# A step's transposes in two halves, with half of the products behind each, and the products half a step later

## Chip, cores, metric

One core of a Trainium2 chip. The metric is device time in microseconds; the kernel before takes 1659.14 us (median of three runs, 1657.83 to 1659.40).

## What is computed

A decoder block of a perceiver: `x` is 8 batches x 64 rows x 2048, the context 8 x 1601 x 2048. All in float32.

```python
x = x + xattn(layernorm(x), ctx)        # a = q @ ctx.T; softmax(a) @ ctx
x = x + attn(layernorm(x), w_q, w_k, w_v, w_o)   # causal, 32 heads, 8 kv heads
x = x + ffn(layernorm(x), A_w, B_w, Wq_w, keys)  # 64 gated experts of rank 8
```

The change lies in the first line. Keys and values of this cross attention are both the context itself: for the scores it is needed transposed, for the products (softmax times context) as it lies in memory.

## The kernel before

**Tiling.** A batch is two stages: `x = 0` with 833 keys (six tiles of 128 and an odd one of 65) and `x = 1` with 768 (six tiles). A stage is four steps (`PER`), one for each 512 columns of the model dimension; a step is four chunks (`CHUNKS`) of 128 columns. There are 64 steps (`STEPS`) that transpose and score, and a few behind them. Below, steps of a batch are numbered 0 to 7.

**What TensorE (PE) does in a step**, in the order in which it is written in `cross_tensor` (line 610 on):
- four chunks of transposes (`transpose_chunk`, L623), six or seven tiles each, into one of two PSUM places (`u % UNITS`). ACT copies columns 0 to 511 to `xa_ct` (L442), DVE the others (L577). A chunk waits until the copies of the chunk two before it are through (`first_copied`, `second_copied`). Some steps transpose more in the same places: step 5 the exponentials of the stage just scored (`xa_expo`, L638, and `xa_odd_e`, L641) and step 1 likewise, step 7 the next batch's queries (`xa_xq`, L635), which wait for `q_ready`;
- the products (`product`, L690) that `product_steps` puts in this step;
- the scores (`scores`, L664, L668), which wait for the copies of this step's chunks.

A product of the order ("use") is one key tile for each of two halves of the keys, which go to the two halves of the array's columns. Stage 0 has 14 uses, stage 1 has 12, in four groups (512 columns each) that accumulate in banks 6 and 7. The uses of a stage are spread over four steps that begin one step (`PV_AT`) after its last scores. `GROUP_STEP` is the step of a group's last use, and the work of the other engines is placed by it through `groups_before(t, ago)`.

**The other engines**, each with its own loop over the steps, all in order:
- ACT: four copies of chunks; in step 0 and 4 of a batch the softmax (L424, L427); for each group of this step the copy of the first stage's sum to `xa_acc` (L457) or of the upper half to `xa_low` (L460); in `OUT_NORM_AT` the finished rows are normalized (L466).
- DVE: four copies of chunks (and L579 for exponentials and queries); maxima (L507 to L515); statistics of the previous step's group (`out_row_stats`, L556); in `OUT_LINKS_AT` the chain for the finished rows (L561, L213 to L219, L590); for the next batch's queries statistics in steps 2 to 5 (L480), a chain whose halves stand in steps 5 and 6 (L486, L213 to L219; `CHAIN_AT`), and in step 6 (`NORM_AT`) the four multiplies L490, the last of which sets `q_ready`; last the epilogue of this step's group: `rescale` (L532), `fold` (L538), `finish` (L548). A link waits for the link before it.
- SyncE (SP): for each group of the previous step the reload of its piece of context for the next batch (L363), stores of finished rows, loads of `xq` and `xr`.

```python
            for gh, c in groups_before(t, 1):
                if gh % HALVES == 1 and gh // HALVES != B - 2:
                    out_row_stats(gh // HALVES, c)
            if t in OUT_LINKS_AT:
                some(out_links(), 11)
```

The decoder behind it (attention and experts, some 1,050 us) starts with transposes of the finished rows (L1677) and isn't touched.

Of the kernel before, what the change touches and what calls it, by code (L numbers as in the profile page):

```python
# [37 lines left out]
SIDES, JOINT = 2, 3  # L38
# [3 lines left out]
STAGES = HALVES * B  # L42
CHUNKS, UNITS = 4, 2
PER = DC // CHUNKS
STEPS = STAGES * PER
PV_AT = 1
# [34 lines left out]
def product_steps():  # L81

    at, step_of = {}, {}
    for h in range(STAGES):
        n = USES_OF[h % HALVES]
        for i in range(n):
            t = PER * (h + 1) + PV_AT + (i * PER // n if h < STAGES - 1 else i // JOINT)
            at.setdefault(t, []).append((h, i))
            step_of[h, i] = t
    return at, step_of  # L90


USE_AT, USE_STEP = product_steps()
GROUP_STEP = {(h, c): USE_STEP[h, GROUP_END[h % HALVES][c]] for h in range(STAGES) for c in range(NCOL)}
GROUPS_AT = {}
# [30 lines left out]
def chunk_no(t, u):  # L126

    return CHUNKS * min(t, STEPS) + u


def chunks_at(t):

    return range(CHUNKS if t < STEPS else JOINT if t == E_LAST else 0)


def copies_until(what, h, j):

    return next(chunk_no(t, u) for (t, u), v in SIDE.items() if (what, h, j) in v) + 1
# [83 lines left out]
def cross_attention(nc, stack, x_rows, ctx, x1, x1_norm, ps, ident, ident_ready, x1_tiles, x1_ahead, row_bn,  # L222
# [95 lines left out]
    def side(a):  # L318
        return slice(a * LQ, (a + 1) * LQ)

    def group_bank(h, c):

        return ps[:, (6 if h < STAGES - 1 or c < 2 else 4) + c % 2, :]
# [286 lines left out]
    def cross_tensor(pe):  # L610
        pe.wait_ge(ident_ready, 2)

        def transpose_chunk(t, u):
            stage, i = divmod(t, PER)
            b, x = divmod(stage, HALVES)
            n = chunk_no(t, u)
            if n >= UNITS:
                pe.wait_ge(first_copied, n - 1)
                pe.wait_ge(second_copied, n - 1)
            if u == 0:  # L620
                pe.wait_ge(raw_in[x][i], 16 * len(loads[x]) * (b + 1))
            for k, p in enumerate(TILES[x]):
                ins = pe.transpose(ps_t[:, u % UNITS, k * P:k * P + p], raw[x][0:p, i, k, u * P:(u + 1) * P], ident[0:p, 0:p])  # L623
            side_step(t, u, ins).then_inc(t_done, 1)

        def last_chunk(u):
            if u >= UNITS:
                pe.wait_ge(second_copied, chunk_no(STEPS, u) - 1)
            side_step(E_LAST, u, None).then_inc(t_done, 1)

        def side_step(t, u, ins):
            for (what, n, k), (dst, part) in zip(SIDE.get((t, u), []), side_parts(t, u)):
                if what == "q":
                    pe.wait_ge(q_ready, n + 1)
                    ins = pe.transpose(part, xq[:, k * P:(k + 1) * P], ident[0:LQ, 0:LQ])  # L635
                elif what == "e":
                    pe.wait_ge(e_ready, 3 * (n // HALVES) + (1 if n % HALVES == 0 else 3))
                    ins = pe.transpose(part, expo[:, k * P:(k + 1) * P], ident[:])  # L638
                else:
                    pe.wait_ge(e_ready, 3 * (n // HALVES) + 2)  # L640
                    ins = pe.transpose(part, odd_e[:], ident[0:LQ, 0:LQ])  # L641
            return ins

        def first_queries():
            pe.wait_ge(q_ready, 1)
            for c in range(DC):
                ins = pe.transpose(ps_q[:, c * LQ:(c + 1) * LQ], xq[:, c * P:(c + 1) * P], ident[0:LQ, 0:LQ])
            ins.then_inc(first_q_done, 1)
            pe.wait_ge(first_q_out, 1)

        def scores(t):
            stage, i = divmod(t, PER)
            b, x = divmod(stage, HALVES)
            bank = stage % 2
            if i == 0 and stage >= 2:
                pe.wait_ge(e_ready, 3 * ((stage - 2) // HALVES) + (1 if x == 0 else 3))
            for u in range(CHUNKS):
                pe.wait_ge(first_copied, chunk_no(t, u) + 1)
                pe.wait_ge(second_copied, chunk_no(t, u) + 1)
                g = CHUNKS * i + u  # L660
                first, last = g == 0, g == DC - 1
                q = q_t[:, b % 2, g, :]
                keys = ct[:, u, :]
                ins = [pe.matmul(ps_s[side(a), bank, 0:MAIN], q, keys[:, a * MAIN:(a + 1) * MAIN], start=first, stop=last)  # L664
                       for a in range(SIDES)]
                if x == 0:
                    a = u % 2
                    ins[a] = pe.matmul(ps_s[side(a), bank, MAIN:MAIN + ODD], q, keys[:, ODD_AT:ODD_AT + ODD], start=False,  # L668
                                       stop=g >= DC - 2, skip_group_check=True)
            if i == PER - 1:  # L670
                for a in range(SIDES):
                    ins[a].then_inc(s_done[a], 1)

        def product(h, n):
            b, x = divmod(h, HALVES)
            what, c, j = USES[x][n]
            first = x == 0 and c % 2 == 1
            if c == 0:
                pe.wait_ge(second_copied, copies_until("odd" if what == "odd" else "e", h, j))
            if what == "joint" and j == 0 and (c == 0 or x == 1 or c % 2 == 0) or what == "odd":  # L680
                free_bank(h, c + 1 if what == "odd" else c)
            for a in range(SIDES):
                if what == "odd":
                    pe_lhs, col, tile = e_odd[0:ODD, :], c + a, raw[x][0:ODD, c + a, 6, :]
                    start, stop = a == 1, a == 0
                else:
                    pe_lhs, col, tile = e_t[:, x, j, side(a)], c, raw[x][:, c, a * JOINT + j, :]
                    start = j == 0 and not (first and a == 1)
                    stop = j == JOINT - 1 and not (x == 0 and c % 2 == 0 and a == 0)
                pe.matmul(group_bank(h, col)[side(a), :], pe_lhs, tile, start=start, stop=stop).then_inc(pv_done[a], 1)  # L690

        def free_bank(h, c):

            ph, pc = (h, c - 2) if c >= 2 else (h - 1, c + 2)
            if ph < 0 or h == STAGES - 1 and c >= 2:
                return
            pe.wait_ge(first_out if ph % HALVES == 0 else finished, NCOL * (ph // HALVES) + pc + 1)

        for t in range(ALL_STEPS):
            for u in chunks_at(t):  # L700
                if t < STEPS:
                    transpose_chunk(t, u)
                else:
                    last_chunk(u)
                if t == 0 and u == UNITS - 1:
                    first_queries()
            for h, n in USE_AT.get(t, []):
                product(h, n)
            if t < STEPS:
                scores(t)  # L710

    over = Over(pv_done, uses_before(STAGES), finished, ahead_in, stored)
    return over, (cross_sync, cross_scalar, cross_vector, cross_tensor)


# [1298 lines left out]
```

## Time and profile before

| | |
|---|---|
| median of 3 runs | 1659.14 us |
| profiled execution | 1658.72 us, its span 1656.9 us |
| PE busy, weight loads (PEld) busy | 1623.7 us (98%), 1202.1 us (73%) |
| DVE, ACT, POOL busy | 780.6, 554.5, 473.4 us |
| chain that ended last | PE 96%, DVE 2%, ACT 1% |

A row of the timeline has the start, the duration and the instructions that were merged into it; since matrix multiplies overlap, the length of a run on PE is read as the difference of the starts of this row and the next. A float32 product or score leaves two records for each instruction, a transpose one. The page's chain of waits follows the work that ended last: its share by engine tells which engine a saved microsecond must come from.

### The profile page before, as it was taken

The page shows a single profiled execution, that of the slowest core. Times are in us where ns is not written, and L with a number is a line of the kernel's source. Part 1 is how long each engine was busy: PE and PEld are TensorE (multiplying, and loading weights), DVE is VectorE, ACT ScalarE, POOL GpSimd, SP SyncE. Part 2 cuts the span into 40 slices and gives each one's busy share as a digit, 9 for nine tenths or more (in the row PEclk, how much of TensorE's full clock was granted, in tenths as well). Part 3 has the DMA queues.
Part 4 walks back from the last instruction along what each step waited for, and adds up shares of the span by engine and source line. Part 5 has one row for each costly group of instructions (what it writes and reads, how often), then busy time and mean ns, then how long its engine had stood idle before and what let it go on. Part 6 is the DMA issues. An engine that isn't in the chain of part 4 may idle for free.

```text
span 1656.9 us, 22594 instructions
## 1 busy us (share of the span) xinstructions
PE 1623.7 (98%) x8893; PEld 1202.1 (73%) x8893; DVE 780.6 (47%) x1331; ACT 554.5 (33%) x790; POOL 473.4 (29%) x161
## 2 busy tenths in 40 slices
PE   7999999999999979999999999999999999999999
PEld 5565655556555548888888888888888888887877
DVE  3454646455464450154374445543744460248323
ACT  2333334343434332232332332333423323222221
POOL 0000000000011003346466366465663663440010
PEclk9999999999999989999999999999999999999999
DMA  9456666666667523323323333233233342220023
GB/s 341 152 200 211 200 211 213 201 226 196 227 215 234 188 92 130 99 77 102 102 77 100 101 101 101 73 105 101 73 104 102 101 145 83 79 100 27 26 77 127
DMA packets 178888, 224.58 MB, mean 136 GB/s; under 512 B 4240, under 2 KB 102544, under 8 KB 176048
## 3 DMA queue, kind: packets, MB, share of 16 engines
q1 hardware_dynamic: 178816, 223.56, 42.1%
q8 instruction: 52, 0.85, 0.2%
q14 instruction: 20, 0.16, 0.0%
HBM read 212.54 MB, written 11.01 MB: 135 GB/s over the span
## 4 chain that ended last, share of the span: by engine, by line
PE 96%; DVE 2%; ACT 1%; issue 0%; DMA 0%; SPq 0%; DVEq 0%
PE ps L742 14%; PE ps L744 14%; PE ps L743 14%; PE ps L623 12%; PE ps L690 11%; PE ps L664 10%; PE ps L1772 5%; PE ps L1774 5%; PE ps L1773 5%; PE ps L1712 2%; PE ps L1865 1%; PE ps L1737 1%; PE ps L635 1%; PE ps L1677 0%; DMA xa_raw_a<-in_ctx 0%
## 5 line engine op out<-in xcount | busy, mean ns | idle before, releaser
L742 PE MATMUL ps<-h_hi,w_hi 128*128 128x512 f32 x800 | 316.0, 395 | 0.1
L744 PE MATMUL ps<-h_hi,w_lo 128*128 128x512 f32 x800 | 312.0, 390 | 0.0
L743 PE MATMUL ps<-h_lo,w_hi 128*128 128x512 f32 x800 | 311.6, 390 | 0.0
L1170 POOL TENSOR_TENSOR w_lo<-raw,w_hi 128x2048 fp32r<-128x2048 f32 (+1 forms) x52 | 212.7, 4096 | 335.6 <-ACT w_hi L1235 293.9
L577 DVE COPY xa_ct<-ps 128x321 f32<-128x321 f32 (+1 forms) x256 | 117.4, 458 | 212.1 <-PE ps L623 137.2
L442 ACT ACTIVATE xa_ct<-ps 128x512 f32<-128x512 f32 x256 | 152.8, 598 | 187.3 <-PE ps L623 116.3
L664 PE MATMUL ps<-xa_ct,xa_q_t 128*64 128x384 f32 x1024 | 184.5, 490 | 0.0
L742 PEld LDWEIGHTS ps<-h_hi,w_hi 128*128 128x128 f32 x800 | 150.4, 188 | 35.0 <-issue 5.1
L744 PEld LDWEIGHTS ps<-h_hi,w_lo 128*128 128x128 f32 x800 | 150.2, 188 | 32.0
L743 PEld LDWEIGHTS ps<-h_lo,w_hi 128*128 128x128 f32 x800 | 150.4, 188 | 30.0
L1524 DVE TENSOR_TENSOR rows<-rows,ps 128x512 f32<-128x512 f32 x168 | 115.5, 688 | 116.1 <-PE ps L1774 116.1
L1164 POOL TENSOR_TENSOR w_lo<-raw,w_hi 128x2048 fp32r<-128x2048 f32 x2 | 9.1, 4540 | 507.5 <-ACT w_hi L1059 507.5
L1176 POOL TENSOR_TENSOR w_lo<-wo_t_sum,w_hi 128x1024 fp32r<-128x1024 f32 x48 | 115.0, 2406 | 69.7 <-ACT w_hi L1264 69.7
L1772 PE MATMUL ps<-w_hi,wo_a_hi 128*128 128x512 f32 x336 | 131.4, 391 | 0.0
L1773 PE MATMUL ps<-w_lo,wo_a_hi 128*128 128x512 f32 x336 | 130.8, 389 | 0.0
L664 PEld LDWEIGHTS ps<-xa_ct,xa_q_t 128*64 128x64 f32 x1024 | 72.3, 137 | 69.0 <-issue 68.6
L623 PE MATMUL ps<-ident,xa_raw_a 128*128 128x128 f32 (+1 forms) x896 | 109.1, 274 | 12.3 <-DMA xa_raw_a<-in_ctx 10.3
L1176 POOL TENSOR_TENSOR w_lo<-raw,w_hi 128x1024 fp32r<-128x1024 f32 x36 | 96.4, 2692 | 63.1 <-ACT w_hi L1264 63.1
L623 PEld LDWEIGHTS ps<-ident,xa_raw_a 128*128 128x128 f32 (+1 forms) x896 | 97.2, 143 | 23.1 <-issue 14.5
L1311 ACT ACTIVATE sa_q_t<-ps 128x512 f32<-128x512 f32 x32 | 19.1, 598 | 263.3 <-PE ps L744 263.3
L623 PE MATMUL ps<-ident,xa_raw_b 128*128 128x128 f32 x768 | 102.6, 278 | 1.5 <-ACT xa_ct L442 0.4
L623 PEld LDWEIGHTS ps<-ident,xa_raw_b 128*128 128x128 f32 x768 | 82.5, 141 | 23.9 <-issue 14.3
(238 smaller groups left out, 2322.7 us busy)
## 6 DMA issues: line engine op xcount, KB each, us to landing
xa_raw_a<-in_ctx SPq DMA_DIRECT2D x32, 1536.0 KB
xa_raw_b<-in_ctx SPq DMA_DIRECT2D x32, 1536.0 KB, 6.7
raw<-in_L_attn_w_q SPq DMA_DIRECT2D x32, 1024.0 KB, 5.9
raw<-in_L_attn_w_o SPq DMA_DIRECT2D x30, 1024.0 KB, 5.0
raw<-in_L_attn_w_k SPq DMA_DIRECT2D x8, 1024.0 KB, 5.7
raw<-in_L_attn_w_v SPq DMA_DIRECT2D x8, 1024.0 KB, 5.7
xa_xq<-in_x SPq DMA_DIRECT2D x8, 512.0 KB, 5.1
xa_raw_a<-in_ctx SPq DMA_DIRECT2D x32, 128.0 KB
```

Of the source, the lines that this page charges most:

```text
L442: act.activation(ct[:, u, 0:512], ps_t[:, u % UNITS, 0:512], ACT.Copy).then_inc(first_copied, 1)
L577: ins = dve.tensor_copy(ct[:, u, 512:width(t)], ps_t[:, u % UNITS, 512:width(t)])
L623: ins = pe.transpose(ps_t[:, u % UNITS, k * P:k * P + p], raw[x][0:p, i, k, u * P:(u + 1) * P], ident[0:p, 0:p])
L664: ins = [pe.matmul(ps_s[side(a), bank, 0:MAIN], q, keys[:, a * MAIN:(a + 1) * MAIN], start=first, stop=last) for a in range(SIDES)]
L690: pe.matmul(group_bank(h, col)[side(a), :], pe_lhs, tile, start=start, stop=stop).then_inc(pv_done[a], 1)
L742: pe.matmul(out, hi, mov_hi, start=first, stop=False)
L743: pe.matmul(out, hi, mov_lo, start=False, stop=False)
L744: return pe.matmul(out, lo, mov_hi, start=False, stop=last)
L1170: pool.tensor_tensor(w_lo[:, n % 2, part], raw[:, n % 2, part], w_hi[:, n % 2, part].bitcast(F32), ALU.subtract).then_inc(w_lo_done, 1)
L1176: pool.tensor_tensor(half_slot(w_lo, p), half_source(p), half_slot(w_hi, p).bitcast(F32), ALU.subtract).then_inc(w_lo_done, 1)
L1772: pe.matmul(out, st_hi, hi[:, wc], start=first and k == 0, stop=False, skip_group_check=True)
L1773: pe.matmul(out, st_hi, lo[:, wc], start=False, stop=False, skip_group_check=True)
```

## The change

`product_steps` counts in half steps ("slots"), begins one slot later and keys `USE_AT` by step and half; `USE_STEP`, and with it `GROUP_STEP`, is the slot halved, rounded down. The loop of PE takes the products of half 0 behind chunk 1 and those of half 1 behind chunk 3.

```diff
@@ product_steps
-            t = PER * (h + 1) + PV_AT + (i * PER // n if h < STAGES - 1 else i // JOINT)
-            at.setdefault(t, []).append((h, i))
-            step_of[h, i] = t
+            slot = 2 * (PER * (h + 1) + PV_AT) + 1 + (i * 2 * PER // n if h < STAGES - 1 else 2 * (i // JOINT))
+            at.setdefault(divmod(slot, 2), []).append((h, i))
+            step_of[h, i] = slot // 2
@@ cross_tensor
         for t in range(ALL_STEPS):
-            for u in chunks_at(t):
-                if t < STEPS:
-                    transpose_chunk(t, u)
-                else:
-                    last_chunk(u)
+            for u in range(CHUNKS):
+                if u in chunks_at(t):
+                    if t < STEPS:
+                        transpose_chunk(t, u)
+                    else:
+                        last_chunk(u)
                 if t == 0 and u == UNITS - 1:
                     first_queries()
-            for h, n in USE_AT.get(t, []):
-                product(h, n)
+                if u % 2:
+                    for h, n in USE_AT.get((t, u // 2), []):
+                        product(h, n)
             if t < STEPS:
                 scores(t)
```

On PE, a step 0 (the first step of a batch, here the second batch) before, from the previous scores to the next:

```order
L664 MATMUL ps<-xa_ct,xa_q_t 64x384 x8
L623 MATMUL ps<-ident,xa_raw_a 128x128 x6
L623 MATMUL ps<-ident,xa_raw_a 128x65
L623 MATMUL ps<-ident,xa_raw_a 128x128 x6
L623 MATMUL ps<-ident,xa_raw_a 128x65
L623 MATMUL ps<-ident,xa_raw_a 128x128 x6
L623 MATMUL ps<-ident,xa_raw_a 128x65
L623 MATMUL ps<-ident,xa_raw_a 128x128 x6
L623 MATMUL ps<-ident,xa_raw_a 128x65
L690 MATMUL ps<-xa_raw_a,xa_e_t 64x512 x6
L664 MATMUL ps<-xa_ct,xa_q_t 64x384 x2
```

and in the change:

```order
L664 MATMUL ps<-xa_ct,xa_q_t 64x384 x8
L623 MATMUL ps<-ident,xa_raw_a 128x128 x6
L623 MATMUL ps<-ident,xa_raw_a 128x65
L623 MATMUL ps<-ident,xa_raw_a 128x128 x6
L623 MATMUL ps<-ident,xa_raw_a 128x65
L690 MATMUL ps<-xa_raw_a,xa_e_t 64x512 x2
L690 MATMUL ps<-xa_raw_a,xa_e_odd 64x512 x2
L623 MATMUL ps<-ident,xa_raw_a 128x128 x6
L623 MATMUL ps<-ident,xa_raw_a 128x65
L623 MATMUL ps<-ident,xa_raw_a 128x128 x6
L623 MATMUL ps<-ident,xa_raw_a 128x65
L690 MATMUL ps<-xa_raw_a,xa_e_t 64x512 x4
```

Two uses (four instructions) stand behind the second chunk and two behind the fourth.

On DVE, step 6 of the second batch, from the last links of step 5 to the first copy of step 7 before (`xa_rs_w` is the chain of the next batch's queries):

```order
L216 TENSOR_SCALAR xa_rs_w<-xa_rs_w 64x1
L218 TENSOR_SCALAR xa_rs_w<-xa_rs_w 64x1
L577 COPY xa_ct<-ps 128x256 x4
L219 TENSOR_SCALAR xa_rs_w<-xa_rs_w 64x1
L218 TENSOR_SCALAR xa_rs_w<-xa_rs_w 64x1
L219 TENSOR_SCALAR xa_rs_w<-xa_rs_w 64x1
L218 TENSOR_SCALAR xa_rs_w<-xa_rs_w 64x1
L219 TENSOR_SCALAR xa_rs_w<-xa_rs_w 64x1
L490 TENSOR_SCALAR xa_xq<-xa_xq,xa_mv,xa_rs_w 64x512 x4
L577 COPY xa_ct<-ps 128x256
```

and in the change, from the epilogue that now ends step 5 (`xa_out_rs` is the chain of the finished rows; it goes on for seven rows more):

```order
L532 SCALAR_TENSOR_TENSOR ps<-xa_acc,xa_alpha,ps 128x512
L538 TENSOR_TENSOR ps<-ps,xa_low 64x512
L548 SCALAR_TENSOR_TENSOR xa_xr<-ps,xa_total,xa_xr 64x512
L577 COPY xa_ct<-ps 128x256 x4
L556 BN_STATS xa_out_bn<-xa_xr 64x6
L561 BN_AGGR xa_out_mv<-xa_out_bn 64x2
L213 TENSOR_SCALAR xa_out_rs<-xa_out_mv 64x1
L214 TENSOR_SCALAR xa_out_rs<-xa_out_rs 64x1
```

and its end, up to the same copy of step 7:

```order
L219 TENSOR_SCALAR xa_out_rs<-xa_out_rs 64x1
L590 TENSOR_SCALAR xa_out_rs<-xa_out_mv,xa_out_rs 64x1
L219 TENSOR_SCALAR xa_rs_w<-xa_rs_w 64x1
L218 TENSOR_SCALAR xa_rs_w<-xa_rs_w 64x1
L219 TENSOR_SCALAR xa_rs_w<-xa_rs_w 64x1
L218 TENSOR_SCALAR xa_rs_w<-xa_rs_w 64x1
L219 TENSOR_SCALAR xa_rs_w<-xa_rs_w 64x1
L490 TENSOR_SCALAR xa_xq<-xa_xq,xa_mv,xa_rs_w 64x512 x4
L577 COPY xa_ct<-ps 128x256
```

The statistics L556 and the chain L561 to L590 of the finished rows moved from step 5 into step 6, ahead of the queries' last links.

## Rows read from the trace of the kernel before

**Rows 1.** The page: busy time of the engines over the span

```profile
PE 1623.7 (98%) x8893; PEld 1202.1 (73%) x8893; DVE 780.6 (47%) x1331; ACT 554.5 (33%) x790; POOL 473.4 (29%) x161
```

**Rows 2.** Table by stretches: length, busy PE, PEld, DVE, ACT, POOL; clock, DMA share, GB/s

```profile
320.00:400.00 80.00, 79.80 (x555) 47.52 (x551) 44.74 (x110) 32.04 (x60) 0.00 (x0) 1.00 0.65 213
...
600.00:620.00 20.00, 10.68 (x61) 9.42 (x60) 14.40 (x30) 7.95 (x13) 0.00 (x0) 0.74 0.41 112
...
700.00:1657.00 957.00, 947.82 (x4490) 782.59 (x4488) 447.01 (x509) 294.11 (x315) 434.67 (x143) 1.00 0.29 90
```

**Rows 3.** List of waits up to 660 us: us in total, times, longest

```profile
PEld ps L623 <- ACT xa_ct L442: 12.4, 56, 0.6
```

**Rows 4.** Timeline of PE, steps 4 and 5: start, duration, instructions

```profile
337.27 2.75 PE L664 MATMUL ps<-xa_ct,xa_q_t 128*64 128x384 f32 x16
339.95 0.87 PE L623 MATMUL ps<-ident,xa_raw_b 128*128 128x128 f32 x6
340.66 0.27 PE L638 MATMUL ps<-ident,xa_expo 128*128 128x128 f32 x1
340.77 0.82 PE L623 MATMUL ps<-ident,xa_raw_b 128*128 128x128 f32 x6
341.42 0.27 PE L638 MATMUL ps<-ident,xa_expo 128*128 128x128 f32 x1
341.79 0.85 PE L623 MATMUL ps<-ident,xa_raw_b 128*128 128x128 f32 x6
```

**Rows 5.** Timeline of PE, step 6 and the head of step 7

```profile
349.70 3.09 PE L623 MATMUL ps<-ident,xa_raw_b 128*128 128x128 f32 x24
352.72 2.79 PE L690 MATMUL ps<-xa_raw_a,xa_e_t 128*64 128x512 f32 x12
...
358.02 0.88 PE L623 MATMUL ps<-ident,xa_raw_b 128*128 128x128 f32 x6
358.83 0.46 PE L635 MATMUL ps<-ident,xa_xq 64*128 64x64 f32 x4
359.22 0.88 PE L623 MATMUL ps<-ident,xa_raw_b 128*128 128x128 f32 x6
```

**Rows 6.** Timeline of PE, the last two steps with products of stage 14

```profile
580.10 2.79 PE L690 MATMUL ps<-xa_raw_a,xa_e_t 128*64 128x512 f32 x12
582.73 1.03 PE L690 MATMUL ps<-xa_raw_a,xa_e_odd 65*64 65x512 f32 x4
583.59 2.75 PE L664 MATMUL ps<-xa_ct,xa_q_t 128*64 128x384 f32 x16
586.17 2.74 PE L690 MATMUL ps<-xa_raw_a,xa_e_t 128*64 128x512 f32 x12
588.84 0.44 PE L638 MATMUL ps<-ident,xa_expo 128*128 128x128 f32 x2
```

**Rows 7.** Timeline of DVE, step 6: last copy, last links, the queries' multiplies

```profile
352.82 0.42 DVE L577 COPY xa_ct<-ps 128x256 f32<-128x256 f32 x1 [0.23 <-PE ps L623]
353.17 0.20 DVE L219 TENSOR_SCALAR xa_rs_w<-xa_rs_w 64x1 f32<-64x1 f32 x1
...
354.48 1.90 DVE L490 TENSOR_SCALAR xa_xq<-xa_xq,xa_mv,xa_rs_w 64x512 f32<-64x512 f32 x4
```

**Rows 8.** Timeline of DVE, step 5: statistics and chain of the finished rows, and what follows

```profile
344.11 0.68 DVE L556 BATCH_NORM_STATS2 xa_out_bn<-xa_xr 64x6 f32<-64x512 f32 x1
344.81 0.26 DVE L561 BATCH_NORM_AGGREGATE xa_out_mv<-xa_out_bn 64x2 f32<-64x24 f32 x1
...
347.58 0.68 DVE L480 BATCH_NORM_STATS2 xa_bn<-xa_xq 64x6 f32<-64x512 f32 x1
```

**Rows 9.** Timeline of DVE, head of step 5, behind the epilogue of step 4

```profile
341.04 0.41 DVE L577 COPY xa_ct<-ps 128x256 f32<-128x256 f32 x1
```

**Rows 10.** Timeline of ACT, end of the softmax in step 4

```profile
338.21 0.19 ACT L427 ACTIVATION_READ_ACCUMULATOR xa_odd_e<-xa_odd_s,xa_neg_max 64x1 f32 x1
```

**Rows 11.** The page: DMA issues of the context's pieces, last the us to landing

```profile
xa_raw_b<-in_ctx SPq DMA_DIRECT2D x32, 1536.0 KB, 6.7
```

## The prediction

> **What bounds the kernel now.** I read the page first: TensorE (PE) is busy 98% of the span [rows 1]. The table by stretches then tells where that holds: in the middle of the cross attention PE is busy 79.8 of 80 us, VectorE (DVE) 44.7, ScalarE (ACT) 32.0, at a granted clock of 1.00; the only long pause is at 600 to 620 us, where the decoder begins; the stretch behind 700 us has the other 948 us of PE and isn't touched by the change [rows 2]. So each 0.1 us that PE's queue gains or loses between about 50 and 590 us goes straight into the time, and work of DVE or ACT costs nothing until PE waits for it. The list of waits has little to win: weight loads of L623 (the transposes) wait 12.4 us in 56 pieces for ACT's copy [rows 3].
>
> I call the steps of a batch 0 to 7 (step number modulo 8). Within a step the timeline of PE has three runs: transposes, products, scores. Products come in pairs of matrix multiplies that run side by side, and every f32 product leaves two records, so "x12" is six products, three uses of the order. Lengths below are differences of starts.
>
> **What is removed.** Chunk 2's transposes overwrite the bank of chunk 0, whose copy has just begun. In step 5 the next transpose comes 0.37 us after the last of chunk 1 (341.42 to 341.79), where 0.11 is usual (340.66 to 340.77) [rows 4]: 0.26 us lost. In step 6 a run of 24 takes 3.02 us; 24 x 0.109 is 2.62, a first one that is 0.06 slow and a last one that is 0.09 slow (below) make 2.77, so 0.25 is the wait [rows 4, 5]. The 56 waits average 0.22 [rows 3]. Step 7 has none: the queries' transposes lengthen each chunk to 1.20 us [rows 5], and the copy is through. In the change half of the products (0.9 to 1.8 us) lies between chunks 1 and 2 and covers the copy (0.6 on ACT). Steps 6 to 63 have products on both sides, 58 steps, 7 of them of kind 7. Gain: 51 x 0.23 = **11.7 us**. Chunk 0 and 1 of the next step and the scores have cover as before: behind chunk 3 still come one or two uses and, for the bank, the scores.
>
> **What is added: a change of tile shape.** The transposes use the array as 128x128, products and scores as 128x64. A run of scores takes 2.58 us where products follow (583.59 to 586.17) and 2.68 where transposes follow (337.27 to 339.95): 0.10 for going over to transposes [rows 4, 6]. Six transposes at the head of a run take 0.71, the next six 0.65: 0.06 [rows 4]. The six before the queries, which have another shape too, take 0.81 = 0.65 + 0.06 + 0.10: some 0.09 for leaving [rows 5]. A product run of 12 records takes 2.63, four more take 0.86, so 12 should take 2.58: 0.05 for the first pair [rows 6]. Together 0.30 us for one more change to products and back. The nearest row of products followed by transposes directly is 586.17 to 588.84, 2.67 against 2.58, with a wait in it: at most 0.09, so the 0.10 fits. In kind 7 the shape changes between chunks anyhow, so only 0.15 is new. 51 x 0.30 + 7 x 0.15 = **16.3 us**. Bounds: from 0.15 a step (the sequencer hides half) to 0.40, 8 to 21 us; I take 0.30, as it is the sum of four lengths that stand there in each step. The Trainium skill (TensorEngine Tiling (Array Packing), Key Properties) says that "changing tiling mode (not just tile) drains the TensorE", which speaks against this change. It gives no length; the rows agree with a cost at each such place. Without such a drain the sum below would be 16.3 less, 1658, and that is one of the rivals.
>
> So the new order by itself is -11.7 + 16.3 = **+4.6 us**.
>
> **What is moved on DVE.** The slots start half a step late, but the step in which a group of products ends is rounded up: all groups but those of the last stage count as ending a full step later, in its first half. ACT, DVE and SP are placed by that number, so the epilogues (L532, L538, L548), statistics and stores of a batch move one step. Mostly this fits: the epilogue now follows chunk 3's copy at once instead of waiting for the products. It doesn't in step 6. There the normalization of the next batch's queries must end before step 7's queries are transposed. Now DVE does in step 6, behind the copy that starts at 352.82, the last links (from 353.17) and four multiplies (1.90 us from 354.48), done at 356.38; PE reaches the queries at 358.83, so there are 2.45 us of slack [rows 5, 7]. The change puts the finished rows' last statistics and their thirteen-instruction chain ahead of these links, which had been done in step 5: 344.11 to 347.58, **3.47 us** [rows 8]. And PE comes earlier: behind chunk 3 stand two uses (1.77) instead of three (2.63), 0.86 less cover. 3.47 + 0.86 - 2.45 = 1.88, with the semaphore 1.9 us of idle PE. It happens where both chains meet, at steps 14, 22, ..., 54, six times (the first batch has no finished rows, the last two take no such chain): **+11.4 us**. Bounds: 6 x 1.0 (DVE's gaps between links shrink) to 6 x 2.5, 6 to 15 us.
>
> **What else moves, at nothing.** Step 5: the epilogue of step 4 ends on DVE 1.09 us into step 5's transposes (341.04 against 339.95) [rows 4, 9]; with 0.86 less cover it will be 1.95. Chunk 0's two copies then end near 2.6; PE wants that bank at 1.58 for two chunks + 0.09 + 0.91 for one use + 0.10 = 2.68. Hidden, by a tenth of a microsecond; if the cover fails, chunk 2 waits, 7 times. The softmax (on ACT to 338.4, some 3.8 us behind chunk 3 [rows 10]) is wanted 5.2 us behind it. SP: each reload of a context piece is issued half a step later; it is wanted at least a step and a half (13 us) after the issue and took 6.7 us in the median [rows 11]; hidden. The end: steps 61 to 63 hold two uses less and steps 64 and 65 two more, one of which fills the wait for the last softmax, and one shape change is added: about 0. The decoder's start waits for the same last products.
>
> **Sum.** The profiled execution took 1658.72 us (span 1656.9), 0.4 below the median of 1659.14. 1658.7 - 11.7 + 16.3 + 11.4 = 1674.7: **1675 us**, 1.0% slower. About 0.2% (3.3 us) is what a measurement of this kernel can tell from no change.
>
> **Rivals.**
> - *Queries in time.* If DVE's chain in step 6 is shorter or starts earlier than I place it, only the shape changes remain: 1658.7 + 4.6 = 1663. For it: nothing in the rows; against it: DVE works in order, and the chain waits for each link. 8%.
> - *Shape changes free.* The loads of weights run ahead of the multiplies, and half a microsecond of product may hide the change: 1658.7 - 11.7 + 11.4 = 1658, no change. Against it: the scores don't hide it today. 7%.
> - *Faster.* Both prices are lengths between starts, which may hold waits that aren't the chain's own. If leaving and re-entering the transposes costs below 0.05 us, and the links run back to back (some 0.20 a link and no statistics behind a copy) so that the queries are ready 5.3 us behind chunk 3 and not 7.1, what remains is the gain at chunk 2: 1658.7 - 11.7 = 1647. The point is the step-6 chain: above 5.3 us it can't be. 4%.
> - *More late work.* The tenth of spare time in step 5 isn't there, DVE is late by 0.5 to 1 us at chunk 2, seven times, or the idle time in step 7 is 2.5: 1679 to 1685. 14%.
> - My forecast, own range 1670 to 1679: 67%.
>
> **Range.** From the first rival's lower side, 1661, to 1681; it leaves out the two fast cases and the upper part of the late one, some 2 in 10. Faster by over 0.2%: 5%; within: 7%; slower: 88%.
>
> **What would show it.** In the changed trace: the waits of L623 for ACT's copy are gone; product runs of x4 and x8 between transposes, the former 0.91 long, and a step of kind 6 takes some 0.05 more than 8.32, a step 7 1.9 + 0.15 more; L635 waits for DVE L490 six times, near 1.9 us each; the cross attention's end (L1677 at 600.27) lies 16 us later, and the decoder behind it is as long as before. No idle before L635 would make the second half of the sum wrong; product runs followed by transposes at 0.86 would make the first half wrong.

## The result, and the profile after

The changed kernel takes 1676.96 us (median of four runs, 1675.67 to 1682.03) against 1659.27 (median of four, 1657.83 to 1659.42): a ratio of 1.0107 between the medians and of 1.0115 over all runs, 95% interval 1.0103 to 1.0127. It is slower by 1.0 to 1.3%; 1675 was forecast, with a range of 1661 to 1681. The profiled execution is the longest of the four and lies just above that range, 1682.03 us with a span of 1680.1 and a mean granted clock of 0.991; the others have 0.995 and 0.996, the kernel before 0.997.

The page of the changed kernel, engines over the span:

```profile
PE 1636.6 (97%) x8893; PEld 1199.4 (71%) x8893; DVE 777.2 (46%) x1331; ACT 552.1 (33%) x790; POOL 473.6 (28%) x161
```

Against [rows 1] the same instructions keep PE busy 12.9 us longer, and some 10 us of idle time came on top. Lines behind the loop are two higher than before: L1679 is the old L1677.

The timeline of PE in step 6 and step 7 of a batch in the changed kernel (start, duration, instructions, idle time before and its releaser):

```profile
204.81 1.53 PE L623 MATMUL ps<-ident,xa_raw_b 128*128 128x128 f32 x12
206.26 1.08 PE L690 MATMUL ps<-xa_raw_a,xa_e_t 128*64 128x512 f32 x4
207.17 1.03 PE L690 MATMUL ps<-xa_raw_a,xa_e_odd 65*64 65x512 f32 x4
208.13 1.53 PE L623 MATMUL ps<-ident,xa_raw_b 128*128 128x128 f32 x12
209.59 1.94 PE L690 MATMUL ps<-xa_raw_a,xa_e_t 128*64 128x512 f32 x8
211.36 2.75 PE L664 MATMUL ps<-xa_ct,xa_q_t 128*64 128x384 f32 x16
214.04 0.87 PE L623 MATMUL ps<-ident,xa_raw_b 128*128 128x128 f32 x6
216.80 0.46 PE L635 MATMUL ps<-ident,xa_xq 64*128 64x64 f32 x4 [1.88 <-DVE xa_xq L490]
...
218.38 1.08 PE L690 MATMUL ps<-xa_raw_a,xa_e_t 128*64 128x512 f32 x4
219.39 0.88 PE L623 MATMUL ps<-ident,xa_raw_b 128*128 128x128 f32 x6
...
221.78 1.94 PE L690 MATMUL ps<-xa_raw_a,xa_e_t 128*64 128x512 f32 x8
```

Step 6 is 9.23 us long (204.81 to 214.04). It was 8.32 [rows 5], but now holds four uses and not three; less 0.86 for the fourth it is 8.37, 0.05 more, as forecast. The wait of 0.25 is missing, and one more change to products and back costs 0.30: the two runs of 12 transposes take 2.91 together instead of 3.02 for the run of 24, and the two runs of products take 3.64 (1.87 and 1.77) instead of 3.48 (2.62 and 0.86). A single use between transposes takes 1.01 (218.38 to 219.39), not the 0.86 of [rows 6]. In step 7 the queries start 2.76 us into the step (214.04 to 216.80) where they started 0.81 in [rows 5]: 1.95 us.

DVE in the same stretch of the changed kernel shows why:

```profile
209.70 0.42 DVE L577 COPY xa_ct<-ps 128x256 f32<-128x256 f32 x1 [0.23 <-PE ps L623]
210.04 0.68 DVE L556 BATCH_NORM_STATS2 xa_out_bn<-xa_xr 64x6 f32<-64x512 f32 x1
...
213.52 0.20 DVE L219 TENSOR_SCALAR xa_rs_w<-xa_rs_w 64x1 f32<-64x1 f32 x1
...
214.84 1.91 DVE L490 TENSOR_SCALAR xa_xq<-xa_xq,xa_mv,xa_rs_w 64x512 f32<-64x512 f32 x4
```

The finished rows' statistics and chain take 3.48 us (210.04 to 213.52; 3.47 in [rows 8]) ahead of the queries' links, and the multiplies end at 216.75, 7.16 behind the start of the products behind chunk 3. The list of waits of the changed kernel, 40 to 640 us, counts six such places:

```profile
PE ps L635 <- DVE xa_xq L490: 9.7, 6, 1.9
PE ps L623 <- DMA xa_raw_b<-in_ctx: 1.5, 1, 1.5
```

Five are 1.88 long and one 0.3: there PE first waited 1.5 us for a piece of context, while DVE went on. In all six steps the queries start 1.95 us later than before.

One thing is new. The table by stretches of the changed kernel (length, busy PE, PEld, DVE, ACT, POOL; clock, DMA share, GB/s) has the granted clock low right behind some of these waits:

```profile
301.00:366.00 65.00, 65.00 (x441) 36.97 (x439) 33.57 (x85) 24.85 (x50) 0.00 (x0) 1.00 0.71 225
366.00:378.00 12.00, 10.12 (x54) 6.07 (x52) 5.99 (x18) 2.38 (x5) 0.00 (x0) 0.72 0.11 40
```

and its timeline of PE shows what that costs:

```profile
369.37 0.69 PE L635 MATMUL ps<-ident,xa_xq 64*128 64x64 f32 x4 [1.88 <-DVE xa_xq L490]
369.99 1.54 PE L623 MATMUL ps<-ident,xa_raw_b 128*128 128x128 f32 x6
371.46 0.69 PE L635 MATMUL ps<-ident,xa_xq 64*128 64x64 f32 x4
372.07 1.97 PE L690 MATMUL ps<-xa_raw_a,xa_e_t 128*64 128x512 f32 x4
373.98 1.54 PE L623 MATMUL ps<-ident,xa_raw_b 128*128 128x128 f32 x6
```

Six transposes take 1.47 (369.99 to 371.46) instead of 0.80, one use 1.91 instead of 1.01: that is the lower of the two levels, 1.2 GHz (the table has 0.50 of full speed over 448 to 452 us, in the second such fall). Step 7 up to its second product run took 10.69 us here (366.62 to 377.31) and 7.74 at the full clock (214.04 to 221.78): 2.95 us more. This trace has two such falls and a shorter one near 294 us (1.5 us), 7.4 us in all.

The best yardstick is the stretch from the second step's first transposes to the decoder's first transposes, called the phase below. It leaves out the decoder and also the head of the execution, where PE waits for the first piece of context and which the theory doesn't speak of: the second step starts between 21.43 and 24.73 us in the nine traces of this case. Before:

```profile
23.76 3.28 PE L623 MATMUL ps<-ident,xa_raw_a 128*128 128x128 f32 x28
...
600.27 1.09 PE L1677 MATMUL ps<-ident,ahead 128*128 128x128 f32 x8
```

Changed:

```profile
23.19 3.28 PE L623 MATMUL ps<-ident,xa_raw_a 128*128 128x128 f32 x28
...
623.35 1.09 PE L1679 MATMUL ps<-ident,ahead 128*128 128x128 f32 x8
```

The phase takes 576.51 us before and 600.16 in the change, 23.65 more. 4.6 for the split, 11.7 (6 x 1.95) for the queries, where 11.4 were forecast, and 7.4 for the clock make 23.7.

### The profile page after: what moved, and what is told of

The parts are those of the page before. It is cut to its first block, busy times and chain, and to the rows that moved or that the text cites. A ratio compares the mean times of both kernels' runs of the same rounds, so it can differ in the third digit from the quotient of the medians.

```text
span 1680.1 us, 22594 instructions
## 1 busy us (share of the span) xinstructions
PE 1636.6 (97%) x8893; PEld 1199.4 (71%) x8893; DVE 777.2 (46%) x1331; ACT 552.1 (33%) x790; POOL 473.6 (28%) x161
## 4 chain that ended last, share of the span: by engine, by line
PE 93%; DVE 4%; ACT 1%; issue 1%; DMA 0%; SPq 0%; DVEq 0%
PE ps L744 14%; PE ps L746 14%; PE ps L745 14%; PE ps L623 12%; PE ps L690 11%; PE ps L664 9%; PE ps L1774 5%; PE ps L1776 5%; PE ps L1775 5%; PE ps L1714 2%; PE ps L1867 1%; PE ps L1739 1%; PE ps L635 1%; DVE xa_xq L490 1%; DMA xa_raw_a<-in_ctx 0%
## 5 line engine op out<-in xcount | busy, mean ns | idle before, releaser
L744 PEld LDWEIGHTS ps<-h_hi,w_hi 128*128 128x128 f32 x800 | 150.3, 188 | 35.1 <-issue 5.2
L623 PEld LDWEIGHTS ps<-ident,xa_raw_a 128*128 128x128 f32 (+1 forms) x896 | 96.7, 142 | 41.7 <-issue 20.8
L623 PE MATMUL ps<-ident,xa_raw_a 128*128 128x128 f32 (+1 forms) x896 | 109.2, 273 | 12.7 <-DMA xa_raw_a<-in_ctx 11.0
L623 PEld LDWEIGHTS ps<-ident,xa_raw_b 128*128 128x128 f32 x768 | 85.5, 144 | 45.1 <-issue 25.6
L623 PE MATMUL ps<-ident,xa_raw_b 128*128 128x128 f32 x768 | 106.1, 284 | 1.9 <-DMA xa_raw_b<-in_ctx 1.5
```

The source lines that it names most:

```text
L744: pe.matmul(out, hi, mov_hi, start=first, stop=False)
```

## The experiments

The theory has three terms: waits at chunk 2 gone (-11.7), one more change of tile shape and back in each step (+16.3), queries late behind the finished rows' chain on DVE (+11.7). Each experiment takes one away, doubles it, or puts a rival in its place. "The phase" is the yardstick above, 576.5 us before; each run's second step starts at the first of the two times given with it, the decoder at the second.

**e1: the queries first on DVE.** Changed order, two blocks of `cross_vector` exchanged:

```diff
+            if b < B - 1:
+                if at == STATS_AT[0]:
+                    dve.wait_ge(xq_in, 16 * (b + 2))
...
             for gh, c in groups_before(t, 1):
                 if gh % HALVES == 1 and gh // HALVES != B - 2:
                     out_row_stats(gh // HALVES, c)
             if t in OUT_LINKS_AT:
                 some(out_links(), 11)
...
-            if b < B - 1:
-                if at == STATS_AT[0]:
-                    dve.wait_ge(xq_in, 16 * (b + 2))
...
```

> The changed order, but on DVE the next batch's query work of a step (statistics, links, the four multiplies) stands ahead of the finished rows' statistics and links. My theory (three terms: waits at chunk 2 gone, -11.7; shape changes, +16.3; queries late behind the finished rows' chain, +11 to 12): the queries are ready 3.66 us behind the start of step 6's last products and wanted at 5.25, so L635 waits for nothing; the other chain then ends 2.7 us into step 7, where chunk 2 may wait some 0.1 us, six times. 1659.3 + 4.6 + 0.6 = 1664 (1662 to 1666), and a granted clock as before (0.997). Rival: the idle time before L635 comes from the moved loads or from ACT and only looks like DVE's; then it stays and the time is 1675 to 1678.

Measured: 1665.99 us, ratio 1.0049 (1.0033 to 1.0066) to 1658.10 in the same session, and a granted clock of 0.997 in the profiled run. Its timelines of PE and DVE:

```profile
213.71 0.87 PE L623 MATMUL ps<-ident,xa_raw_b 128*128 128x128 f32 x6
214.52 0.46 PE L635 MATMUL ps<-ident,xa_xq 64*128 64x64 f32 x4
...
216.10 1.08 PE L690 MATMUL ps<-xa_raw_a,xa_e_t 128*64 128x512 f32 x4
217.22 0.85 PE L623 MATMUL ps<-ident,xa_raw_b 128*128 128x128 f32 x6
...
606.63 1.09 PE L1679 MATMUL ps<-ident,ahead 128*128 128x128 f32 x8
```

```profile
211.03 1.91 DVE L490 TENSOR_SCALAR xa_xq<-xa_xq,xa_mv,xa_rs_w 64x512 f32<-64x512 f32 x4
212.86 0.68 DVE L556 BATCH_NORM_STATS2 xa_out_bn<-xa_xr 64x6 f32<-64x512 f32 x1
...
216.34 0.41 DVE L577 COPY xa_ct<-ps 128x256 f32<-128x256 f32 x1
```

The wait before L635 is gone and with it the falls of the clock, by an exchange on DVE alone: it was DVE's order. The chain now ends 2.6 us into step 7, and chunk 2 waits 0.11 us (1.12 between 216.10 and 217.22 instead of 1.01), as expected. The phase (24.73 to 606.63) is 5.4 us longer than before; 5.2 were expected. The time as a whole is 7.9 above its session's 1658.10, at the upper end of the 1662 to 1666 expected: in the two traces 1.0 of the difference stands ahead of the second step and 0.9 behind the decoder's start. In the 5.4, 0.5 is one wait that I had booked at nothing. A step later in its numbering, the last piece of context for the last batch is issued by SP behind the decoder's first weights, not ahead of them. SP's timeline of e1:

```profile
497.28 0.37 SPq L1057 DMA_DIRECT2D raw<-in_L_attn_w_q  x1
497.75 1.43 SPq L363 DMA_DIRECT2D xa_raw_b<-in_ctx  x1
```

and of the kernel before:

```profile
483.39 0.37 SPq L363 DMA_DIRECT2D xa_raw_b<-in_ctx  x1
...
491.97 0.37 SPq L1055 DMA_DIRECT2D raw<-in_L_attn_w_q  x1
```

The transposes that need it wait 0.42 us at 509.18 in e1. The 1.5 us in the changed kernel are the same wait.

**e2: later, but not split.** The changed kernel with

```diff
-                if u % 2:
-                    for h, n in USE_AT.get((t, u // 2), []):
+                if u == CHUNKS - 1:
+                    for h, n in USE_AT.get((t, 0), []) + USE_AT.get((t, 1), []):
                         product(h, n)
```

> The products of the changed order, half a step later and with the epilogues where the change has them, but both halves of a step stand behind chunk 3, so there is no shape change more than before. My theory: the 56 waits at chunk 2 are back, no switch is added, and since four uses (3.49 us) stand behind chunk 3 in step 6, the queries are late by 3.47 - (2.45 + 0.86), 0.2 us with the semaphore, six times: 1659.3 + 1.3 = 1660.6 (1659 to 1662). Rival: being half a step late costs by itself (reloads, epilogues, the end of the phase), and the split is innocent: 1665 or more.

Measured: 1661.33 us (ten runs, 1658.06 to 1665.08), ratio 1.0020 (1.0010 to 1.0029); the phase (22.81 to 600.93) is 1.6 us longer than before, 1.3 expected. Its list of waits:

```profile
PEld ps L623 <- ACT xa_ct L442: 12.6, 56, 0.6
...
PE ps L635 <- DVE xa_xq L490: 0.9, 6, 0.2
```

The 56 waits of [rows 3] are back with 12.6 us, and the queries are late by 0.15 us six times. So the half step alone costs 1.6 us in the phase, 0.9 of it these six waits, and 1.7 to 4.8 in the time as a whole; three of the ten runs had a lower clock (0.993 to 0.995), and what the rest of the difference is stays open. Moving the epilogues by a step is harmless as long as enough products stand behind chunk 3.

**e3: split, but not later.** The changed kernel with

```diff
-            slot = 2 * (PER * (h + 1) + PV_AT) + 1 + (i * 2 * PER // n if h < STAGES - 1 else 2 * (i // JOINT))
+            slot = 2 * (PER * (h + 1) + PV_AT) + (i * 2 * PER // n if h < STAGES - 1 else 2 * (i // JOINT) + 1)
```

> The split without the half step of delay: slots begin one earlier, so groups end in the steps of the kernel before and the chains on DVE stand as before. My theory: switches and removed waits as in the change (+4.6), no wait for the queries; but the first use of a stage now stands behind chunk 1 of step 5 and needs the exponentials' copy, which DVE makes only after the epilogue of step 4; with one use (0.91) and the scores (2.68) behind chunk 3 the epilogue ends 2.9 us into step 5, the copy at 3.5, and PE wants it at 1.67: 1.8 us, seven times, 12.7. 1659.3 + 4.6 + 12.7 = 1676.6 (1673 to 1680), with waits of L690 for DVE L579. Rival: the delay is not needed, the exponentials are there in time: 1664.

Measured: 1677.85 us, ratio 1.0116 (1.0099 to 1.0133); the phase (23.37 to 617.43) is 17.5 us longer than before, 17.3 expected. Its timeline of PE in a step 5:

```profile
198.67 0.27 PE L638 MATMUL ps<-ident,xa_expo 128*128 128x128 f32 x1
200.66 1.94 PE L690 MATMUL ps<-xa_raw_a,xa_e_t 128*64 128x512 f32 x8 [1.72 <-DVE xa_e_t L579]
```

The first use waits for the exponentials' copy, six times for 1.72 us and the last time for 1.13, 11.4 in all where 12.7 were expected; in return a step 1 is 0.17 us longer than in the changed kernel, seven times, with no wait of PE in the list, which stays open. So the delay by half a step belongs to the split: without it the split costs the same as with the late queries, by another wait. The 1.72 against the 1.8 expected agrees with the way in which DVE's backlog was reckoned.

**e4: first half of the products behind chunk 0.** e1 with

```diff
-                if u % 2:
+                if u in (0, CHUNKS - 1):
```

> As e1, but the first half of the products stands behind chunk 0 and not behind chunk 1: the same number of shape changes, and no product between the chunks 1, 2 and 3. My theory: chunk 3 now waits for chunk 1's copy as chunk 2 did before, so the gain of 11.7 us is gone and the price of 16.3 stays: 1659.3 + 16.3 + 0.6 = 1676 (1673 to 1678). Rival 1: the split covers the copies wherever it stands: as e1, 1664. Rival 2: shape changes cost nothing: 1659 to 1660.

Measured: 1676.04 us, ratio 1.0106 (1.0089 to 1.0123); the phase (23.20 to 616.28) is 16.6 us longer than before. Its timeline of PE in a step 6:

```profile
207.87 1.08 PE L690 MATMUL ps<-xa_raw_a,xa_e_odd 65*64 65x512 f32 x4
208.88 2.44 PE L623 MATMUL ps<-ident,xa_raw_b 128*128 128x128 f32 x18
211.25 1.94 PE L690 MATMUL ps<-xa_raw_a,xa_e_t 128*64 128x512 f32 x8
```

The run of 18 takes 2.37; 18 x 0.109 + 0.06 + 0.09 is 2.11, so 0.26 is the wait, now at chunk 3. Against e1 the phase grew by 11.2 us: that is what half of the products at the right place are worth, 11.7 by the forecast. The price of the shape changes, 16.3 by the forecast, is left in full.

**e5: quarters.** e1 with

```diff
-            slot = 2 * (PER * (h + 1) + PV_AT) + 1 + (i * 2 * PER // n if h < STAGES - 1 else 2 * (i // JOINT))
-            at.setdefault(divmod(slot, 2), []).append((h, i))
-            step_of[h, i] = slot // 2
+            slot = 4 * (PER * (h + 1) + PV_AT) + 3 + (i * 4 * PER // n if h < STAGES - 1 else 4 * (i // JOINT))
+            at.setdefault(divmod(slot, 4), []).append((h, i))
+            step_of[h, i] = slot // 4
...
-                if u % 2:
-                    for h, n in USE_AT.get((t, u // 2), []):
-                        product(h, n)
+                for h, n in USE_AT.get((t, u), []):
+                    product(h, n)
```

> As e1, but the products are dealt out in quarters, one behind each chunk (one use each, some places empty): 134 places where a transpose follows a product, against 60 in the change and 1 before. My theory: each is a change of tile shape and back, 0.30 us, 0.15 in step 7: 119 x 0.30 + 14 x 0.15 = 37.8, less the 11.7 of waits: 1659.3 + 26.1 = 1685 (1680 to 1690), product runs of x4 with 1.01 us each. Rival: the price is one for a step that is split at all (or the chip overlaps short runs): as e1, some 1664.

Measured: 1684.55 us, ratio 1.0159 (1.0142 to 1.0176), which is 25.8 above the 1658.73 of that session, and the phase (22.98 to 625.36) is 25.9 us longer than before; 26.1 expected. Its timeline of PE:

```profile
207.43 0.87 PE L623 MATMUL ps<-ident,xa_raw_b 128*128 128x128 f32 x6
208.24 1.08 PE L690 MATMUL ps<-xa_raw_a,xa_e_t 128*64 128x512 f32 x4
209.24 0.87 PE L623 MATMUL ps<-ident,xa_raw_b 128*128 128x128 f32 x6
210.05 1.08 PE L690 MATMUL ps<-xa_raw_a,xa_e_t 128*64 128x512 f32 x4
```

Each chunk of six is 0.81 long, 0.65 + 0.06 + 0.10, each use 1.00, 0.86 + 0.05 + 0.10: 0.30 for each change and back, however many there are (0.81 - 0.65 and 1.00 - 0.86, as measured). The time grows with their number; the price isn't one for a split step. That it is the shape and not the kind of work is seen in step 7: the queries are transposes too, only 64 rows high, and a run of six takes the same 0.81 ahead of them (358.02 to 358.83 [rows 5]) as here ahead of products, while the exponentials, of the transposes' own shape, add only 0.11 (340.66 to 340.77 [rows 4]).

**e7: the finished rows' chain twice.** The changed kernel with

```diff
                 some(out_links(), 11)
+                some(out_links(), 11)
```

> The changed kernel with the finished rows' chain of eleven links computed twice in step 6 (the same values again). My theory: the queries are later by 2.65 us, six times, +15.9: 1675 + 15.9 = 1691 at the clock of before, and each wait before L635 4.6 us and not 1.95. The granted clock fell for 3.4 to 6.8 us behind three of the six waits in the changed kernel's trace; if these falls come from the waits, longer waits bring more of them: up to six of 6.8 us at half clock, 3.4 us each, so 1691 to 1711. Rival: the wait before L635 is not this chain's: 1677 as the change.

Measured: 1706.34 us (1704.77 to 1706.94), ratio 1.0283 (1.0265 to 1.0300), granted clock 0.985 or 0.986 in all four runs. Its waits (lines one higher) and its table by stretches:

```profile
PE ps L636 <- DVE xa_xq L490: 25.8, 6, 4.5
```

```profile
290.00:305.00 15.00, 11.21 (x70) 5.62 (x66) 11.13 (x39) 3.47 (x6) 0.00 (x0) 1.00 0.47 159
305.00:313.00 8.00, 7.29 (x33) 4.67 (x34) 2.80 (x8) 1.79 (x3) 0.00 (x0) 0.57 0.01 2
```

The wait follows the chain: 4.51 us each and 2.6 more than in the changed kernel (the last comes as 1.2 for a piece of context and 3.3 for the queries). Above 1675.0 (1658.7 + 4.6 + 11.7) this makes 15.9; the other 15 us are put down to the clock, which in this trace fell at all six waits, towards their end or right behind them, for 6.8 us at five of them and 3.4 at the first. By its trace the phase is 46.8 us longer than before (24.51 to 647.85), 14.7 more than 4.6 and 27.5 (6 x 4.58) explain.

**e8: a wait for each bank.** If the gain at chunk 2 is real but a change of shape eats it, the wait must be shortened without one. The kernel before, with its own order, and in `transpose_chunk`:

```diff
-            if n >= UNITS:
-                pe.wait_ge(first_copied, n - 1)
-                pe.wait_ge(second_copied, n - 1)
...
-            for k, p in enumerate(TILES[x]):
-                ins = pe.transpose(...)
+            tiles = list(enumerate(TILES[x]))
+            banks = [(first_copied, tiles[:4]), (second_copied, tiles[4:])]
+            for copied, part in banks if (t, u) in SIDE or (t, u - 2) in SIDE else banks[::-1]:
+                if n >= UNITS:
+                    pe.wait_ge(copied, n - 1)
+                for k, p in part:
+                    ins = pe.transpose(...)
```

> The kernel before, with its own order of transposes, products and scores; only inside a chunk the wait for the two copies is taken apart. A chunk's place is two banks: ACT copies the first (0.60 us), DVE the second (0.42 or 0.49, in steps with exponentials 0.76). Where DVE is the faster, a chunk begins with the tiles of the second bank and waits for DVE alone, then for ACT; in steps with exponentials or queries it begins with the first bank and waits for ACT alone. My theory: the wait at chunk 2 is the slower copy's end and nothing else, and no shape change is needed to shorten it: 16 waits shorter by 0.18, 21 by 0.11, 14 by 0.16, 7.4 us: 1658.7 - 7.4 = 1651 (1649 to 1655), faster than both kernels. Rival: the gap comes from any stop of the queue at a semaphore, however short: then it stays, 1658 to 1660, or grows with the second wait.

Measured: 1652.84 us (five runs, 1650.68 to 1653.93), ratio 0.9962 (0.9947 to 0.9976): faster than both kernels. The waits of the transposes (L625 here) for ACT are 1.9 us in 9 places instead of 12.4 in 56 [rows 3]. Its timeline of PE, step 5 and the head of step 6:

```profile
190.50 0.82 PE L625 MATMUL ps<-ident,xa_raw_b 128*128 128x128 f32 x6
191.16 0.27 PE L641 MATMUL ps<-ident,xa_expo 128*128 128x128 f32 x1
191.36 0.87 PE L625 MATMUL ps<-ident,xa_raw_b 128*128 128x128 f32 x6
...
199.29 2.99 PE L625 MATMUL ps<-ident,xa_raw_b 128*128 128x128 f32 x24
202.21 2.37 PE L693 MATMUL ps<-xa_raw_a,xa_e_t 128*64 128x512 f32 x10
```

Behind the exponentials of chunk 1 the next transpose comes after 0.20 us, not 0.37 [rows 4]; the run of 24 takes 2.92, not 3.02 [rows 5]. The rival, a stop at any wait, falls: there are twice as many waits in the queue, and it is shorter. The phase (21.43 to 591.35) is 6.6 us shorter than before, 7.4 expected; the time as a whole improved by 5.2, in a profiled run whose clock also fell briefly in the decoder (0.91 over 660 to 700 us).

## Why the prediction was right

- **What bounds the kernel**: right. What the phase gained or lost reached the end: from the decoder's start to the end the traces take 1056.6 us before, 1056.8 in the change and 1056.9 to 1057.6 in e1, e2, e4, e5 and e7. Only e3 and e8, whose clock fell in the decoder, take 1058.7 and 1060.8.
- **Removed, -11.7**: the mechanism was right; e4 puts its worth at 11.2, and e8 gets 6.6 us of it without any change of shape. The marker that I named for it was wrong. I wrote that L623's waits for ACT's copy would be gone; the list of the changed kernel has them with 35.1 us in 46 places, e5 with 102.4. They are all of weight loads: behind a run of products the loader is idle while the products stream, and the list puts that down to the semaphore that came last. PE itself has 0.2 us of such waits. The starts on PE tell it, not that row.
- **Shape changes, +16.3**: the four lengths were right (1.01 for one use, 1.46 for a run of 12), and e5 and e4 priced it apart from the gain. Among its signs the prediction had 0.91 for a run of x4 between transposes; that left out its own 0.10 for going over to transposes, which the sum has. Free shape changes, the second rival, fell with e4. That the Trainium skill (TensorEngine Tiling (Array Packing), Key Properties) has the array drain at a change of tiling mode fits all these runs; a change and back costs 0.30 us here.
- **Queries, +11.4**: 1.95 us each against 1.9. e1 removed it, e7 lengthened it by the length of the chain. The rival of queries in time fell; what it would have looked like is e1.
- **What was booked at nothing**: chunk 2 of step 5 held six times out of seven (the use ahead of it takes 1.01 to 1.03) and was late once (1.33); the tenth to spare was no more than that. The reload behind the decoder's first weights didn't: 0.5 to 1.6 us once, hidden under the late queries in the changed kernel. I had reckoned the time from issue to need and not what stood ahead of it in the queue.
- **Missing**: the clock. The forecast counted the idle time in step 7 and nothing behind it. The clock at the lower level cost 7.4 us in the profiled run. The other three runs, with mean clocks of 0.995 and 0.996 against 0.997, have no trace here; at 1675.7 to 1677.2 they leave 0.7 to 2.2 us for it above the 1675.0 of the three terms. That their clock fell behind the same waits is likely but not shown. The profiled run, by itself, would have been above the range by this term.

## What to carry to other kernels

Before work is put between two others to cover a wait, compare the wait with what leaving and re-entering the first kind of work costs; both stand in the timeline as differences of starts. Here 0.23 us was to be gained for 0.30, and the wait could be had more cheaply by waiting for each bank apart. When work of one engine is renumbered, follow each in-order queue of the others: a chain of 3.5 us that was harmless in one step stood ahead of a deadline in the next. And when two traces are compared, take the difference over a stretch and not at one point: the heads of these executions differ by up to 3.3 us (21.43 to 24.73), more than some of the terms that the experiments were to price.

## What the hardware showed that was not expected

- A stop of PE of 1.88 us was followed by a fall of the granted clock to 1.2 GHz at three of the five places where PE stood that long in one trace. In e7 five stops of 4.5 us and one of 3.3 right behind one of 1.2 all came with a fall (five of them for 6.8 us). The six stops of 1.72 us in e3 were followed by none. A fall of 6.8 us cost 2.95 us, more than the stop that went before it.
- Between an f32 transpose at 128x128 and a product at 128x64 the engine loses 0.30 us there and back, in four parts (some 0.10 at each change, 0.06 on the first transpose and 0.05 on the first product behind it), the same whether a step has one such pair or three.
